# Graph aggregation with indirect gathers on one core: each chunk gathered once, ring places read from registers, third pass written out

## The reference

```python
xn = layernorm(x)
msg = xn[src]                                   # gather, one row of 256 per edge
agg = segment_sum(msg, dst, n)                  # the aggregation of this document
gnn = relu(xn @ W_self + agg / max(deg, 1) @ W_neigh + b)
q, k, v = split(xn @ Wqkv); k = softmax(k, over nodes)
mix = (q @ (k^T v)) * sigmoid(gelu(ln(xn) @ Wg1 + bg1) @ Wg2 + bg2) @ Wproj + bproj
x = x + gnn + mix
# then a graph attention over 131072 other edges, which weights two of four experts per node
x = x + ffn(layernorm(x), edge_index)
```

## Time and profile before

| what | value |
|---|---|
| median of 3 runs | 2320.95 us (2315.45 to 2323.26) |
| the profiled execution's own time | 2314.14 us |
| its span in the profile | 2312.2 us |
| mean granted clock of TensorE | 0.874 of full speed |
| busy: TensorE / VectorE / ScalarE / GpSimd | 78% / 59% / 38% / 67% |
| `aggregate` in the span | about 107 to 1215 us |

### The profile page before, as it was taken

One profiled execution on the slowest core, in us unless ns is written; L12 is line 12 of the kernel. 1 busy time (PEld: TensorE's weight loads), 2 busy tenths in 40 slices (PEclk: granted clock), 3 DMA queues, 4 the chain that ended last, 5 costly groups with the idle time before them and its releaser, 6 DMA issues. The chain is left out here.

```text
span 2312.2 us, 26858 instructions
## 1 busy us (share of the span) xinstructions
PE 1802.0 (78%) x7430; PEld 1240.1 (54%) x7430; DVE 1364.8 (59%) x2596; ACT 888.4 (38%) x1939; POOL 1544.3 (67%) x1560
## 2 busy tenths in 40 slices
PE   4669998887777777777555599999999999981435
PEld 3545555555445445445435466767666776751423
DVE  6457554466767767667569633435545353654578
ACT  2433645554454443453314333232323223231234
POOL 2277777777777777777760377777777777777530
PEclk8879999998989889899775599999999999995555
DMA  5463333344454544544637832231312313225564
GB/s 178 154 224 99 103 101 101 102 141 136 143 154 137 158 139 136 165 132 130 200 94 222 298 93 58 42 82 42 98 42 58 83 42 88 54 83 163 174 194 159
DMA packets 197545, 289.12 MB, mean 125 GB/s; under 512 B 43654, under 2 KB 148067, under 8 KB 196130
## 3 DMA queue, kind: packets, MB, share of 16 engines
q0 software_dynamic: 63536, 121.55, 20.4%
q1 hardware_dynamic: 95458, 121.11, 15.8%
q10 hardware_dynamic: 38416, 44.96, 5.8%
HBM read 201.71 MB, written 85.80 MB: 124 GB/s over the span
## 5 line engine op out<-in xcount | busy, mean ns | idle before, releaser
L804 POOL DMA_INDIRECT ag_msg<-xn_tab,step_src x832 | 840.8, 1011 | 253.6 <-issue 244.0
L1740 POOL DMA_INDIRECT edge_rows<-hx_d,gat_src x648 | 626.2, 966 | 207.1 <-issue 202.0
L825 DVE TENSOR_TENSOR acc<-acc,ag_ps 128x257 f32 x832 | 351.8, 423 | 341.3 <-PE ag_ps L1058 215.2
L1058 PE MATMUL ag_ps<-ag_msg,ag_hot 128*128 128x257 f32 x1664 | 468.9, 425 | 92.7 <-DVE acc L825 39.3
L1058 PEld LDWEIGHTS ag_ps<-ag_msg,ag_hot 128*128 128x128 f32 x1664 | 321.7, 207 | 236.6 <-DVE acc L825 114.1
L1916 PE MATMUL ex_psF<-co_rows 128*128 128x448 f32 x896 | 346.4, 544 | 32.8 <-DMA ex_b<-in_b_dram 24.8
L1231 ACT ACTIVATE gat_self<-iota_row,step_nloc 128x128 f32<-128x128 f32 x832 | 254.4, 388 | 253.9 <-issue 131.4
L1928 PE MATMUL ex_psY<-co_rows 128*128 128x256 f32 x1568 | 345.4, 381 | 7.3 <-ACT co_rows L1975 7.2
L1854 DVE TENSOR_TENSOR hi_one_low<-hi_numbers,hi_low 128x2048 bf16<-128x2048 f32 x64 | 146.3, 2286 | 307.8 <-PE hi_ps L1935 307.7
L1928 PEld LDWEIGHTS ex_psY<-co_rows 128*128 128x128 f32 x1568 | 295.7, 190 | 54.1 <-ACT co_rows L1975 15.1
L1916 PEld LDWEIGHTS ex_psF<-co_rows 128*128 128x128 f32 x896 | 169.4, 191 | 192.6 <-issue 150.6
(11 more groups left out here) (372 smaller groups left out, 2046.5 us busy)
## 6 DMA issues: line engine op xcount, KB each, us to landing
y_d<-co_rows ACTq DMA_DIRECT2D x28, 896.0 KB, 4.1
co_rows<-y_d SPq DMA_DIRECT2D x28, 896.0 KB, 10.4
ag_msg<-xn_tab,step_src POOLq DMA_INDIRECT x832, 2.8
xnT<-base_d SPq DMA_DIRECT2D x7, 1792.0 KB, 10.6
edge_rows<-hx_d,gat_src POOLq DMA_INDIRECT x648
base_d<-xnT ACTq DMA_DIRECT2D x7, 1024.0 KB, 6.0
sums_d<-edge_rows SPq DMA_DIRECT2D x5, 1344.0 KB, 5.7
xg<-in_x_dram SPq DMA_DIRECT2D x7, 896.0 KB, 5.7
```

Of the source, the lines that this page charges most:

```text
L804: pool.indirect_dma_start(msg[:, q, u, 0:D], None, c.xn_tab, bass.IndirectOffsetOnAxis(ap=t.idx[:, at:at + 1], axis=0)).then_inc(s_g[q], 16)
L825: V.tensor_tensor(own, own, bank[u % BANKS][:, 0:ROWW], ALU.add).then_inc(s_acc, 1)
L1058: nc.tensor.matmul(bank[u % BANKS][:, 0:ROWW], hot[:, k, u, :], msg[:, k, u, :], start=True, stop=True).then_inc(s_mm, 1)
L1740: pool.indirect_dma_start(G[:, j % RING, w, :], None, c.hx_d, bass.IndirectOffsetOnAxis(ap=plan.idx[:, at + w:at + w + 1], axis=0)).then_i ...
```

## The change

1. **Each chunk is gathered once.** There are 98 halves of 8 chunks (HALVES), 784 gathers for 832. The step's place in the ring is no longer given by its number: a table row `slot` gives for each step (chunk mod 32) x 257, and TensorE loads it into registers before each group of four or eight steps and reads its rows from there (L1105 to L1109 of the kernel after).
2. **Waits.** GpSimd, before the fifth gather of half h, waits until the gathers of half h - 1 have landed and raises `s_landed`. For h + 1 from 4 on it also loads a number (`freed`) into a register and waits on `s_mm` for it: the step behind which the slots of half h + 1 are free. TensorE waits for `s_landed` at the half of the group's last step, a number that it loads from the row `half`.
3. **Tables.** The rows tile, slot, half and freed lie in one tile `step_table`; `prepare` computes them, writes them out and loads them by four small DMAs instead of one. The sources are transposed by chunk straight from the sorted keys.
4. **Third pass.** The loops of VectorE and TensorE are written out seven times. A block's tile numbers are loaded beside a comparison of the stage before (the argument `meanwhile`), and at a round's end ahead of the drain. A round's turn stands behind the first four steps on TensorE.
5. **Last part.** Four sums move ahead of the wait for the low half of the keys, four steps ahead of a turn.

```diff
-    def compare(self, v, dst, src, dist):
+    def compare(self, v, dst, src, dist, meanwhile=lambda: None):
         nc = self.c.nc
         s, t = pairs(src, dist), pairs(dst, dist)
         nc.vector.tensor_tensor(t[0], s[0], s[1], ALU.min)
         nc.vector.tensor_tensor(t[1], s[0], s[1], ALU.max)
+        loaded = meanwhile()
         v.drain()
-
-    def compare_psum(self, v, dst, src, dist):
+        return loaded
...
         self.nloc = sb("step_nloc", [P, STEP_COLS])
-        self.tile = sb("step_tile", [1, STEP_COLS], I32)
+        table = sb("step_table", [P, STEP_COLS], I32)
+        self.tile, self.slot, self.half, self.freed = (table[i * P // 4:i * P // 4 + 1, :] for i in range(4))
...
-                pool.dma_start(tile_d.rearrange("(g p) -> g p", p=P).bitcast(I32), t_rows[:]).then_inc(s_moved, 16)
+                pool.dma_start(steps_d.rearrange("(g p) -> g p", p=P), t_rows[:]).then_inc(s_moved, 16)
                 pool.wait_ge(s_moved, 64)
-                pool.dma_start(t.tile[:], tile_d.rearrange("(o n) -> o n", o=1).bitcast(I32)).then_inc(s_moved, 16)
-                pool.wait_ge(s_moved, 80)
+                for i, to in enumerate((t.tile, t.slot, t.half)):
+                    pool.dma_start(to, steps_d[i * STEP_COLS:(i + 1) * STEP_COLS].rearrange("(o n) -> o n", o=1)).then_inc(s_moved, 16)
+                pool.dma_start(t.freed[:, 0:P], steps_d[3 * STEP_COLS:ROWS * P].rearrange("(o n) -> o n", o=1)).then_inc(s_moved, 16)
+                pool.wait_ge(s_moved, 128)
...
+                V.tensor_scalar(src_i[:], keys[:], SRC_MASK, None, ALU.bitwise_and)
+                v.drain()
+                V.tensor_scalar(src_f[:], src_i[:], float(N_NODES - 1), None, ALU.min).then_inc(s_src, 1)
+                V.tensor_scalar(freed, ends[:, Q - 1:Q], float(1 + 2 * SBLK), None, ALU.add)
...
+                V.tensor_scalar(slot_i[:], chunk_i[:], SLOTS - 1, None, ALU.bitwise_and)
+                V.tensor_scalar(chunk_i2[:], chunk_i[:], SHALF.bit_length() - 1, None, ALU.logical_shift_right)
+                v.drain()
+                V.tensor_scalar(slot, slot_i[:], float(ROWW), None, ALU.mult)
+                V.tensor_scalar(half, chunk_i2[:], 1.0, None, ALU.add)
...
+                V.tensor_copy(t.idx[:, 0:HALVES * SHALF].rearrange("p (h q) -> p q h", q=Q),
+                              psS[:].rearrange("p (q h) -> p q h", q=Q)[:, :, 0:HALVES])
...
+                    if g == GROUPS - 3:
+                        pe.wait_ge(s_src, 1)
+                        for q in range(Q):
+                            last = nc.tensor.transpose(psS[:, q * P:(q + 1) * P], src_f[:, q * P:(q + 1) * P], c.ident[:])
+                        last.then_inc(s_srcT, 1)
...
-                for half in range(QUART * PAIRS):
-                    q = half % QUART
-
-                    pool.wait_ge(s_mm, half * SHALF + SHALF)
+                def landed(h):
+
+                    pool.wait_ge(s_g[h % QUART], 16 * SHALF * (h // QUART + 1))
+                    pool.sem_inc(s_landed, 1)
+
+                for h in range(HALVES):
+                    q = h % QUART
                     for u in range(SHALF):
-                        at = half * SHALF + u
+                        if h and u == SHALF // 2:
+                            if h + 1 in range(QUART, HALVES):
+
+                                at = h + 1 - QUART
+                                pool.wait_ge(s_mm, pool.value_load(t.freed[:, at:at + 1], min_val=2 * SBLK + 1, max_val=2 * SBLK + STEPS))
+                            landed(h - 1)
+                        at = h * SHALF + u
                         pool.indirect_dma_start(msg[:, q, u, 0:D], None, c.xn_tab,
                                                 bass.IndirectOffsetOnAxis(ap=t.idx[:, at:at + 1], axis=0)).then_inc(s_g[q], 16)
+                landed(HALVES - 1)
...
-                with v.Fori(0, GROUPS) as g:
+                tiles = tiles_of(C_PAIR * 2 * SBLK)
+                for g in range(GROUPS):
                     m = g + 1
                     at = C_PAIR * 2 * SBLK + g * (4 * SBLK)
                     srt.ask(v, m)
-                    tiles = tiles_of(at)
                     sums(at, tiles, 0, 4)
                     shifted(g, 0)
                     v.drain()
                     v.wait_ge(srt.s_turned, 2 * m - 1)
                     scaled(g, 0)
                     srt.across_stage(v, m, 0)
-                    for i in range(1, 4):
+                    for i in range(1, 3):
                         sums(at, tiles, 4 * i, 4 * i + 4)
                         srt.across_stage(v, m, i)
+                    sums(at, tiles, 12, 16)
+                    tiles = srt.across_stage(v, m, 3, lambda: tiles_of(at + SBLK))
                     gated(g, 0)
                     at = at + SBLK
-                    tiles = tiles_of(at)
                     sums(at, tiles, 0, 4)
                     srt.across_stage(v, m, 4)
                     srt.across_stage(v, m, 5)
...
                     shifted(g, 1)
                     v.drain()
                     v.wait_ge(srt.s_turned, 2 * m)
-                    srt.along_stage(v, 0)
+                    tiles = srt.along_stage(v, 0, lambda: tiles_of(at + SBLK))
                     rowed(g, 0, 3)
                     at = at + SBLK
-                    tiles = tiles_of(at)
-                    for i in range(4):
+                    for i in range(3):
                         sums(at, tiles, 4 * i, 4 * i + 4)
                         if i == 0:
                             scaled(g, 1)
                         srt.along_stage(v, 1 + i)
+                    sums(at, tiles, 12, 16)
+                    tiles = srt.along_stage(v, 4, lambda: tiles_of(at + SBLK))
...
                     rowed(g, 1, 2)
+                    if g < GROUPS - 1:
+                        tiles = tiles_of(at + SBLK)
                     v.drain()
                 v.sem_inc(s_sorted, 1)
...
+                block_of(1, SHALF, SBLK - 4)
                 v.wait_ge(s_low_ld, 16)
                 srt.ask(v, MERGES)
-                block_of(1, SHALF, SBLK)
+                block_of(1, SBLK - 4, SBLK)
...
+                    at = half * SHALF + u0
+                    n = u1 - u0
+                    places = nc.values_load_multi_w_load_instructions(
+                        t.slot[:, ds(at, n)], engines=[PE_ENGINE], min_val=0, max_val=(SLOTS - 1) * ROWW,
+                        skip_runtime_bounds_check_because="a remainder by the ring's slots")[1]
                     if u0 == 0:
                         pe.wait_ge(s_hot, half + 1)
-                        pe.wait_ge(s_g[k], 16 * SHALF * p + 16 * SHALF)
+
+                    pe.wait_ge(s_landed, pe.value_load(t.half[:, ds(at + n - 1, 1)], min_val=1, max_val=HALVES))
                     for u in range(u0, u1):
                         pe.wait_ge(s_acc, half * SHALF + u + 1)
-                        nc.tensor.matmul(bank[u % BANKS][:, 0:ROWW], hot[:, k, u, :], msg[:, k, u, :],
+                        nc.tensor.matmul(bank[u % BANKS][:, 0:ROWW], hot[:, k, u, :], ring[:, ds(places[u - u0], ROWW)],
                                          start=True, stop=True).then_inc(s_mm, 1)
...
-                with pe.Fori(0, GROUPS) as g:
-                    srt.turn_from(pe, 0, 2 * g + 1)
+                for g in range(GROUPS):
                     for i in range(2):
                         p = C_PAIR + 2 * g + i
                         steps(p, 0, 0, 4)
+                        if i == 0:
+                            srt.turn_from(pe, 0, 2 * g + 1)
                         hidden(g, i)
...
+                steps(R_PAIR, 3, 0, 4)
                 srt.turn_from(pe, 0, T_LAST + 1)
-                steps(R_PAIR, 3, 0, SHALF)
+                steps(R_PAIR, 3, 4, SHALF)
```

More of the change, by code:

```diff
@@ L52 @@
 STEPS = CH_GNN + TILES - 1
+ROWW = D + 1
+QUART = 4
 SBLK = 16
@@ L57 @@
 STEP_G = STEP_COLS // P
+SLOTS = QUART * SHALF
+HALVES = -(-CH_GNN // SHALF)
+assert STEP_COLS >= HALVES * SHALF and LANE // P == SHALF
 SELF_N = 8192
@@ L209, in compare, with compare_psum @@
         nc.vector.tensor_tensor(t[1], s[0], s[1], ALU.max)
+        loaded = meanwhile()
         v.drain()
-    def compare_psum(self, v, dst, src, dist):
+        return loaded
+    def compare_psum(self, v, dst, src, dist, meanwhile=lambda: None):
         nc = self.c.nc
@@ L243, in ask, with across_stage @@
         v.sem_inc(self.s_ready, 1)
-    def across_stage(self, v, m, i):
+    def across_stage(self, v, m, i, meanwhile=lambda: None):
         nc, c = self.c.nc, self.c
@@ L259, in across_stage, with along_stage @@
             nc.vector.scalar_tensor_tensor(dst[1], src[0], noff, src[1], ALU.add, ALU.max)
+        loaded = meanwhile()
         v.drain()
+        return loaded
     def ask_back(self, v):
         v.sem_inc(self.s_ready, 1)
-    def along_stage(self, v, i):
+    def along_stage(self, v, i, meanwhile=lambda: None):
         if i == 0:
```

(35 more changed lines are left out.)

15 lines of the change are left out of this document (5 added, 10 removed).

## The result

The changed kernel took a median of 2290.53 us (2284.1 to 2296.39, 4 runs), the kernel before 2321.57 beside it (4 runs): a ratio of 0.9882, with an interval from 0.9862 to 0.9902. That is 31.0 us less. The forecast was 44 us less, 2277, in a range from 2252 to 2303. The profiled execution took 2288.34 us, its span is 2286.3.

What follows compares the result with a forecast made beforehand. Gathers were taken to bound passes one and two, with two nearly equal chains in the third; 10.5 + 29.5 + 3.5 = 43.5 us off 2314.14 gives 2270.6, forecast as a 2277 us median, range 2252 to 2303.

Steps and rivals of the forecast that it cites:

- Bound and chains: Third pass: VectorE's own chain shrinks from 83.6 to 77.5 us a round; GpSimd's 80.8 holds, instead of 85.0.
- Rival C: Third pass: VectorE's chain does not shorten, rounds stay 83.6 us, gain 24 us, 2297; chance 0.2.
- How it splits: Gains by stretch: 10.5 us in passes one and two, 29.5 us in the third pass.
- The start: GpSimd's thirteenth gather waits for the first half's landing, until about 135.4 instead of 123.7, costing 11.7 us.
- Rival D: The start costs nothing and landings are never late: gain 60 us, 2261; chance 0.15.
- Waits on GpSimd: Third pass: late landings stall GpSimd, charged 0.7 us a round, 7 us in all at most; waits for free slots zero.
- Register loads: Loads on GpSimd and TensorE are covered by queued work: zero; uncovered, up to 42 us and 236 us.
- rival A: TensorE's register loads are not covered by its queue: 72 us slower, 2393; chance 0.09.
- B: The register loads on GpSimd show, 42 us, so the gain is given back: 2320, no change; chance 0.06.
- The last part: The 96 steps woven with the final merge: 3.5 us gained, from shorter gather waits and four moved sums.
- Waits for gathers at the head: Near the last part's start, waits for gathers (longest 4.60 us) shorten by the faster pace, some 1 us.
- The low half: Last part: four sums move into the 3.20 us wait for the low half, gaining 2.5 us.

Runs made afterwards that it cites:

- the third set: Four kernels on one chip: third pass written out alone 0.9948, once alone 0.9999, first wait after 21 gathers plus loads ahead 0.9792, that with wait at two 0.9911.
- the first two sets: Earlier experiments, each set on one chip, where every kernel took some 20% longer; the kernel before took 2797.88 and 2822.11 us in the median.

## Why the prediction was right, and where it was off

**Bound and chains: right.** The chain by itself measures 75.9 to 79.0 us, 77.3 in the mean (77.5), before 82.6 to 84.2 (83.6), the rounds 79.8 (80.8), held by the gather. The prediction's gain up to the head of the last part, 10.5 + 29.5 = 40.0 us, stands beside 40.7. Rival C falls: the rounds did shorten, and VectorE's product behind the turn (L897), of which the rival feared a wait for TensorE, begins 0.14 us after the operation before it in six of the seven rounds (1.78 in the first).

**How it splits: wrong in part.** The gather of step 288 ends at 474.2 instead of 485.1, 10.9 us earlier (10.5), but VectorE's sum of that step only 4.2 earlier. TensorE goes on in groups of four steps and waits for the half that holds the group's last chunk; since chunks and steps are no longer numbered alike, groups lie across halves. The group of step 260 waited until 455.79 for a half of which it needed one chunk, and so began only 5.0 us earlier than before (460.82). It and its products took 7.0 us; from step 264 on TensorE needs 1.18 us a step to the pass's end, no less than before, and can't use what GpSimd has ready. The third pass uses it: 36.5 us instead of 29.5, of which GpSimd's own gain is 31.3 (from the end of step 288's gather to that of step 736's, 563.8 for 595.1). The two errors of the split are one and the same, so they cancel in the sum.

**The start: right in its price.** The thirteenth gather began at 135.7 instead of 123.7:

```profile
135.72 0.94 POOL L844 DMA_INDIRECT ag_msg<-xn_tab,step_src  x1 [12.87 <-DMA ag_msg<-xn_tab,step_src]
```

Deferring the wait gave back 7.2 us by step 288 of the 12 it cost GpSimd. Rival D is thereby refuted for the change as it stands, and more than half of its 11.7 us were there to be had.

**Waits on GpSimd: right.** Apart from the start, five of its gaps in the third pass stand out, of 0.67 to 1.76 us, 4.2 us over the usual 0.3 together; 5 were charged.

**Register loads.** On GpSimd the 94 take 288 + 147 ns each and show nowhere. On TensorE the places take 508 ns in the median, the landing number 477 + 151; in pass two 8 steps with their products take 9.45 us, the same as before (2 x 4.72), so nothing is left bare, and the third pass's chain came out no longer than worked out. Rivals A and B fall there. Sixteen values on VectorE take 1.10 us as before. The Trainium skill, Runtime: NRT & Kernel Launch (Instruction fetch mechanics), gives about 200 ns for each register, in a passage on the loads that the runtime injects; for these loads, out of an on-chip tile, the trace shows 69 ns a value.

**The last part: the step that failed.** The term was "some 1 us" from waits for gathers and 2.5 from the low half, with TensorE's loads at zero: 3.5 us gained. Measured: 5.3 lost, 8.8 us off. VectorE's sums of steps 744, 752, 760 and 764 in the changed kernel:

```profile
1067.48 0.42 DVE L866 TENSOR_TENSOR acc<-acc,ag_ps 128x257 f32 x1 [6.09 <-PE ag_ps L1109]
...
1078.62 0.42 DVE L866 TENSOR_TENSOR acc<-acc,ag_ps 128x257 f32 x1 [4.81 <-PE ag_ps L1109]
...
1085.66 0.42 DVE L866 TENSOR_TENSOR acc<-acc,ag_ps 128x257 f32 x1 [1.40 <-PE ag_ps L1109]
...
1091.90 0.42 DVE L866 TENSOR_TENSOR acc<-acc,ag_ps 128x257 f32 x1 [3.06 <-PE ag_ps L1109]
```

and in the kernel before, beside the earlier trace rows, those of step 752 and of steps 784 and 800, which stand behind the later turns:

```profile
1115.17 0.42 DVE L825 TENSOR_TENSOR acc<-acc,ag_ps 128x257 f32 x1 [2.78 <-PE ag_ps L1058]
...
1174.22 0.42 DVE L825 TENSOR_TENSOR acc<-acc,ag_ps 128x257 f32 x1 [1.90 <-PE ag_ps L1058]
...
1189.58 0.42 DVE L825 TENSOR_TENSOR acc<-acc,ag_ps 128x257 f32 x1 [1.75 <-PE ag_ps L1058]
```

*Waits for gathers at the head, 5.1 of the 8.8 us.* From the sum of step 736 to that of 752 it takes 22.1 us where 18.0 was: 4.1 lost for 1 gained. The waits of 4.60 and 2.78 us grew to 6.09 and 4.81. A group is eight steps there. That of step 744 has chunks 701 to 707, and TensorE waits for the half of 704 to 711, whose last gather ended at 1060.7 and which landed 5.3 us later; before, half and group were the same eight, though a landing was as late there (5.7 us). From the end of its own chunk's gather, step 744 begins 17.9 us later (14.6 before), step 752 20.3 (13.6):

```profile
1066.12 2.50 PE L1109 MATMUL ag_ps<-ag_msg,ag_hot 128*128 x5 [5.45 <-POOLq L832]
```

One run takes this away: the written-out kernel with 832 gathers has the same last part, with half and group alike. There the two steps begin 14.2 and 13.6 us behind their gathers, as before. Its sums of the two:

```profile
1100.38 0.42 DVE L830 TENSOR_TENSOR acc<-acc,ag_ps 128x257 f32 x1 [7.00 <-PE ag_ps L1067]
...
1109.80 0.42 DVE L830 TENSOR_TENSOR acc<-acc,ag_ps 128x257 f32 x1 [2.85 <-PE ag_ps L1067]
```

So the mixed halves are what holds TensorE back. Yet the stretch takes 21.3 us in that kernel too, and its last part 118.5 where 117.3 was and 2 to 5 less were expected. VectorE comes to step 736 there 13.8 us behind its gather instead of 16.9, and waits the longer. The "some 1 us" was thus wrong even without mixed halves: this stretch goes by the landings, and whoever reaches it sooner waits in it.

*The low half, 0.5 us.* Its wait of 3.20 us did go, as expected, and the wait at step 760 fell from 3.06 to 1.40. But the steps that now stand behind the turn are waited for, 3.06 us at step 764. From step 752 to the end the written-out kernel takes 97.3 us where 99.3 was, so this edit brought 2.0 of its 2.5.

*The loads, 3.2 us.* The changed kernel takes 100.5 us for the same steps. Behind a turn TensorE's queue is empty, and a load of eight places and a number lies bare: the waits of 3.85 and 3.37 us are 1.95 and 1.62 over before. That is rival A in miniature, and the experiment with the loads ahead confirms it for these two waits. The prediction asked what stands in TensorE's queue in passes two and three, but not behind the turns of the last part.

**Behind the aggregation: not foreseen.** In the block that follows, the last 30 us of transposes and products ran at a granted clock of 0.50 instead of 0.61 (window, us, PE busy and so on), here the changed kernel and then the kernel before:

```profile
1244.10:1274.10 30.00, 24.99 (x114) 23.70 (x112) 6.63 (x27) 13.17 (x29) 0.00 (x0) 0.50 0.53 175
```

```profile
1279.50:1309.50 30.00, 19.43 (x112) 18.50 (x112) 11.59 (x34) 12.62 (x28) 4.20 (x5) 0.61 0.67 223
```

A group of 28 small products takes 6.17 us there, at the lower level of 1.2 GHz, and 3.46 or 3.69 in the last two groups of the profile before, and this costs the profiled execution 6 us of the 9.5; 3.6 more went in the blocks behind it, and why stays open. The four kernels of the third set have 0.57, 0.53, 0.50 and 0.58 in that place, among them the written-out one with 832 gathers at 0.50; whether the change shifts the odds of it stays open.

In sum, of the 12.5 us by which the forecast was too large, 8.8 are the last part and, by the estimate made with the result, 4.4 lie behind the aggregation, less 0.7 that the passes gave beyond it.

## What to carry to other kernels

Where two engines' chains are nearly as long as each other, measure each by itself (leave the other's work out) before pricing an edit: here 11 us and 1 us alone made 31 us together. When a wait is added to a stream of queued work, count the work that lies ahead of it in the queue against the slowest answer, not the median one: four gathers were enough here (4.2 us in the third pass), two cost 27 us, and the first answer after a start, 19 us late, is a case of its own. When two numberings that ran alike come apart, look for every wait that is taken in groups, since each group now waits for the later of two blocks.

## What had not been expected of the hardware

In the first two sets VectorE and ScalarE stood still again and again behind matmuls that the profile has as done. VectorE, in the kernel with the written-out third pass:

```profile
250.28 0.69 DVE L209 TENSOR_TENSOR gatsort_keys<-gatsort_keys 128x512 f32<-128x512 f32 x1
263.38 0.42 DVE L830 TENSOR_TENSOR acc<-acc,ag_ps 128x257 f32 x1 [12.42 <-remote]
```
